# Row sums of three units on ScalarE, three exponential buffers, and normalising, products and shifts on GpSimd, in a two-layer attention and feed-forward kernel

## The reference, cut to what matters

```python
x = L0_attn_a_x                                   # (2, 1024, 512) float32, 2 batches
x = x + attn(layernorm(x), W_qkv_a, b_qkv_a, W_out_a, b_out_a)
x = x + ffn(layernorm(x), w_gate, w_up, w_down)
x = x + attn(layernorm(x), w_qkv_b, b_qkv_b, w_proj_b, b_proj_b)
x = x + ffn(layernorm(x), w_gate, w_up, w_down)   # the same weights again

def attn(x, ...):      # 16 heads of 32, causal
    q, k, v = split(x @ W_qkv + b_qkv)
    p = softmax(where(causal, q @ k.T * 32 ** -0.5, -inf))
    return (p @ v) @ W_out + b_out

def ffn(x, ...):       # hidden 2048
    return (silu(x @ w_gate) * (x @ w_up)) @ w_down

def layernorm(x):      # no scale, no shift, eps 1e-5
    return (x - mean(x)) / sqrt(var(x) + eps)
```

## Time and profile before

| | |
|---|---|
| median of 3 runs | 1995.39 us (1995.38 to 1996.1) |
| the profiled execution | 1995.06 us |
| its span, first to last instruction | 1993.3 us |
| mean granted TensorE clock | 0.999 |
| busy share TensorE, VectorE, GpSimd, ScalarE | 98%, 60%, 49%, 40% |
| attention part of iteration 0 | about 18 to 260 us |
| length of one iteration | 493 us |
| records of L1488 with values, with ones | 1536, 1024 |

### The profile page before, as it was taken

The page is one execution under the profiler, slowest core; times in us unless marked ns, Lnnn a source line. Parts: engine busy times, 40 slices in busy tenths (PEclk is TensorE's granted clock), DMA queues, the critical chain, the costliest instruction groups (busy, mean ns, idle before and its releaser), DMA issues.

```text
span 1993.3 us, 27851 instructions
## 1 busy us (share of the span) xinstructions
PE 1957.7 (98%) x10288; PEld 1438.2 (72%) x10288; DVE 1188.4 (60%) x2387; ACT 803.7 (40%) x1478; POOL 983.5 (49%) x767
## 2 busy tenths in 40 slices
PE   6999999999999999999999999999999999999999
PEld 5655588888765558888875656888887565688887
DVE  4777465445578845544567884545456777554544
ACT  2388532221248752222115874222211687332221
POOL 4025369763212537975421252897532225289740
PEclk9999999999999999999999999999999999999999
DMA  5334011121333301311252340111113234012111
GB/s 139 90 86 111 3 55 62 54 64 32 72 82 93 97 21 44 106 45 62 74 138 65 86 97 23 42 64 54 53 32 96 65 86 97 12 53 64 53 43 42
DMA packets 58821, 132.37 MB, mean 66 GB/s; under 512 B 10560, under 2 KB 11584, under 8 KB 58688
## 3 DMA queue, kind: packets, MB, share of 16 engines
q1 hardware_dynamic: 58688, 130.60, 24.3%
HBM read 75.51 MB, written 4.19 MB: 40 GB/s over the span
## 4 chain that ended last, share of the span: by engine, by line
PE 87%; DVE 6%; issue 4%; ACT 2%; POOL 1%; DMA 1%; SPq 0%; DVEq 0%; POOLq 0%; ACTq 0%
PE bank L1488 11%; PE bank L1354 10%; PE bank L1356 10%; PE bank L1355 10%; PE ring L1354 9%; PE ring L1356 9%; PE ring L1355 9%; PE bank L1461 8%; PE ring L1430 8%; PE ring L1345 1%; DVE xn L1051 1%; ACT kq_parts L844 1%; DVE stats L1014 0%; POOL area L657 0%; DVE xt_lo L1060 0%
## 5 line engine op out<-in xcount | busy, mean ns | idle before, releaser
L732 POOL TENSOR_SCALAR_AFFINE_SELECT prob<-prob 128x512 f32<-128x512 f32 x128 | 83.7, 654 | 509.5 <-ACT prob L861 379.2
L861 ACT ACTIVATE prob<-bank 128x512 f32<-128x512 f32 (+1 forms) x512 | 271.8, 572 | 135.0 <-PE bank L1461 125.2
L1168 DVE TENSOR_TENSOR x<-x,bank 128x512 f32<-128x512 f32 x256 | 170.5, 685 | 232.3 <-PE bank L1356 231.7
L657 POOL TENSOR_TENSOR area<-w_stage,area 128x1024 fp32r<-128x1024 f32 x126 | 302.1, 2398 | 10.5
L655 POOL TENSOR_SCALAR area<-w_stage 128x1024 fp32r<-128x1024 f32 x126 | 144.3, 1145 | 301.1 <-PE bank L1356 189.7
L1098 DVE CUSTOM_DVE_ANT_0 xn<-ring,mask_row 128x384 bf16<-128x384 f32 (+7 forms) x384 | 244.9, 661 | 70.1 <-PE ring L1430 65.7
L1354 PE MATMUL ring<-xt_hi,area 128*128 128x512 f32 x672 | 263.9, 393 | 1.3 <-DVE area L1201 1.3
L1356 PE MATMUL ring<-xt_hi,area 128*128 128x512 f32 x672 | 262.1, 390 | 0.0
L1355 PE MATMUL ring<-xt_lo,area 128*128 128x512 f32 x672 | 262.1, 390 | 0.0
L1461 PE MATMUL bank<-area 98*128 98x512 f32 (+3 forms) x768 | 233.2, 372 | 2.3 <-DMA area<-nm_lo 1.4
L1430 PE MATMUL ring<-area 96*128 96x512 f32 (+3 forms) x768 | 221.7, 360 | 2.9 <-DVE row_max L1098 2.1
(11 more groups left out here) (171 smaller groups left out, 3643.9 us busy)
## 6 DMA issues: line engine op xcount, KB each, us to landing
w_stage<-ffn_w SPq DMA_DIRECT2D x96, 512.0 KB, 3.5
area<-kq_parts SPq DMA_DIRECT2D x336, 128.0 KB, 2.4
w_stage<-attn_w SPq DMA_DIRECT2D x32, 512.0 KB, 4.8
area<-attn SPq DMA_DIRECT2D x48, 128.0 KB, 3.3
x<-x_in SPq DMA_DIRECT2D x16, 256.0 KB, 3.9
out<-x SPq DMA_DIRECT2D x16, 256.0 KB, 2.0
bias_rows<-row_bias SPq DMA_DIRECT2D x8, 256.0 KB, 4.2
masked<-x_in SPq DMA_DIRECT2D x6, 256.0 KB, 4.5
```

Of the source, the lines that this page charges most:

```text
L657: pool.tensor_tensor(lo, src, hi.bitcast(F32), ALU.subtract).then_inc(w_split, 1)
L861: act.activation(prob[:, step % PROB_BUFS, h, off:], scores_at(u, j, h), ACT.Exp, scale=SCALE).then_inc(prob_ready, 1)
L1168: dve.tensor_tensor(x[:, t, :], x[:, t, :], row_bank(s, n)[:, :], ALU.add).then_inc(rows_drained, 1)
```

## The change

- `SUMMED` gets unit 1: its row sums move from matmuls with ones to ScalarE, and `ORDER` has 62 instead of 68 letters v, `ACT_ORDER` 48 instead of 32 letters r, 16 of them for unit 1 in the first two strings.
- `PROB_BUFS` 2 to 3, `MASKED_BUFS` 3 to 2.
- The normalise steps of all but the first four tiles go to GpSimd, so do the shift (now four instructions) and the product with the reciprocals for all plain units but the last. In `POOL_ORDER` h is a shift, t a product; d now takes the next of deviations and normalise pairs.
- At the start each x tile has its own semaphore, variance and deviation come for two tiles at a time, the memset L767 stands behind them, and VectorE makes the low parts of the first two weight slots.
- `HEAD_OF_RING` begins with two value tiles instead of the first query and key projections. `EARLY` changes for units 1 and 5, and all strings are written anew.

```diff
-EARLY = {1: 2, 3: 12, 5: 9, 7: 12}
+EARLY = {1: 10, 3: 12, 5: 12, 7: 12}
...
-HEAD_OF_RING = (("q", 0), ("k", 0), ("v", 0), ("v", 1), ("ln1", 2), ("ln1", 3), ("q", 1), ("k", 1))
+HEAD_OF_RING = (("v", 0), ("v", 1), ("q", 0), ("k", 0), ("ln1", 2), ("ln1", 3), ("q", 1), ("k", 1))
...
-PROB_BUFS = 2
-SUMMED = (3, 5)
+PROB_BUFS = 3
+SUMMED = (1, 3, 5)
...
-    "pppppfffffffpfpppppfffffpppffpfpfpffpfpfpffpfpfpfpffpffpffpf",
...
+    "fffffpfppffpppppffffppfpfpffppfpffppfpfpffppfpfpffpfffffff",
...
-    "xxxxxxx",
-    "eexeeeeeeeeexe",
-    "eeeeoeeexeeeeeeeeereereererereereerreer",
...
+    "xxxxxxrrr",
+    "erererexrrexerreerrrrerreexeo",
+    "eeeexeeeeeeeeeereerreerreereereerreererxer",
...
-    "dbbwmmmbmmwmmbmmmmmwmmmbwmmmmmwbaaawammmambmmmbamammdmmwdw",
+    "bbddbdwwmbmbhmbmwbmmmtmmwmhmmbmmmmwtmmmhmaaamtmammmammmawtawdddmmmmdw",
...
-MASKED_BUFS = 3
+MASKED_BUFS = 2
...
-        x_loaded = [sem(f"x_loaded{c}") for c in range(CHUNKS)]
+        x_loaded = [sem(f"x_loaded{t}") for t in range(TT)]
...
+            def normalise_attn(it, u):
+                g, c = unit(u)
+                cols = slice(c * CHUNK, (c + 1) * CHUNK)
+                pool.wait_ge(recip_done, evacuations(it, u) * RECIPS)
+                pool.tensor_tensor(attn[:, g, cols], attn[:, g, cols], recip[:, :], ALU.mult).then_inc(attn_ready, 1)
+            def normalise_pair(it, ln, r):
+                if r >= 2:
+                    pool.wait_ge(ring_full, full(it, (f"ln{ln + 1}", r - 2)))
+                pool.wait_ge(rstd_ready, deviations(it, ln, 2 * r // CT))
+                for t in (2 * r, 2 * r + 1):
+                    src = x[:, t, :] if ln else source_tile(it, t)
+                    pool.tensor_scalar(xn_tile(t), src, mean_var[:, t, 0:1], rstd[:, t:t + 1], ALU.subtract, ALU.mult
+                                       ).then_inc(xn_ready, 1)
+            def shift(it, u):
+                least = row_max[:, u % 2, :]
+                pool.wait_ge(inverse_done, shifts(it, u))
+                pool.tensor_tensor(row_inv[:, :], row_inv[:, :], row_sum[:, :], ALU.mult)
+                pool.tensor_tensor(row_log[:, :], least, row_log[:, :], ALU.subtract).then_inc(shift_step, 1)
+                pool.wait_ge(shift_step, 2 * shifts(it, u) - 1)
+                pool.tensor_tensor(row_log[:, :], row_log[:, :], row_inv[:, :], ALU.subtract).then_inc(shift_step, 1)
+                pool.wait_ge(shift_step, 2 * shifts(it, u))
+                pool.tensor_scalar(least, row_log[:, :], 1.0, None, ALU.add).then_inc(shift_ready, 1)
...
+            for r in range(2):
+                pool.wait_ge(var_ready, r + 1)
+                t = slice(2 * r, 2 * r + 2)
+                pool.tensor_tensor(rstd[:, t], var_eps[:, t], minus_half[:, 0:2], ALU.pow).then_inc(rstd_ready, 1)
+            pool.wait_ge(rstd_ready, 2)
             pool.memset(k_stack[3 * HEAD:3 * HEAD + 2, 1:, :, :].bitcast(F32), 1.0).then_inc(ones_ready, 1)
             pool.wait_ge(ones_ready, 1)
-            inverse_deviation(0, 0, 0)
-            pool.wait_ge(xn_ready, CT)
-            for i in V_SLOTS:
-                hi, lo = w_part(i, slice(0, SLOT))
-                pool.wait_ge(w_hi_done, i + 1)
-                pool.tensor_tensor(lo, w_stage[:, i, :], hi.bitcast(F32), ALU.subtract).then_inc(w_split, 1)
+            pool.wait_ge(w_split, len(V_SLOTS))
...
-                deviations = iter(((0, 1), (1, 0), (1, 1)))
+                norms = iter((("deviation", 0, 1), ("pair", 0, 2), ("pair", 0, 3), ("deviation", 1, 0),
+                              ("pair", 1, 0), ("pair", 1, 1), ("deviation", 1, 1)))
+                shifted = iter(SUMMED)
+                divided = iter([u for u in PLAIN if ATTN_ON_POOL and u != UNITS - 1])
...
+                normalise_pair(it, 1, 2)
+                normalise_pair(it, 1, 3)
                 pool.wait_ge(xn_ready, it * 2 * TT + 2 * TT)
...
+            def first_normalise(r):
+                dve.wait_ge(rstd_ready, r + 1)
+                for t in (2 * r, 2 * r + 1):
+                    dve.tensor_scalar(xn_tile(t), x[:, t, :], mean_var[:, t, 0:1], rstd[:, t:t + 1],
+                                      ALU.subtract, ALU.mult).then_inc(xn_ready, 1)
+            def first_weights_lo(i):
+                hi, lo = w_part(i, slice(0, SLOT))
+                dve.wait_ge(w_hi_done, i + 1)
+                dve.tensor_tensor(lo, w_stage[:, i, :], hi.bitcast(F32), ALU.subtract).then_inc(w_split, 1)
...
-                        if n == RECIPS - 1:
+                        if n == RECIPS - 1 and (v_unit == UNITS - 1 or not ATTN_ON_POOL):
...
-            chunk_stats(0, 0)
-            normalise_pair(0, 0, 0)
-            normalise_pair(0, 0, 1)
+            for t in range(CT):
+                dve.wait_ge(x_loaded[t], 16)
+                tile_stats(t, x[:, t, :])
+                if t % 2:
+                    variances(t + 1, range(t - 1, t + 1))
+            first_normalise(0)
+            first_weights_lo(0)
+            first_normalise(1)
             xt_to_lo(0, 0, 0)
+            first_weights_lo(1)
             xt_to_lo(0, 0, 1)
```

112 lines of the change are left out of this document (50 added, 62 removed).

## The result

The changed kernel takes 2073.69 us (median of 4 runs, 2070.46 to 2075.42), the kernel before 1995.39 (1994.24 to 1996.1). The ratio is 1.0391, 95% interval 1.0374 to 1.0407: 78 us slower, where I had forecast 37 us faster with a range of 1930 to 1986.

What follows compares the result with a forecast made beforehand. TensorE, busy 98% of the span, was taken as the bound, so only removed TensorE work or stops could count. -25 - 4.5 - 6 - 5 + 4 = -36.5 us gave 1958.5 us, range 1930 to 1986.

Steps and rivals of the forecast that it cites:

- (c): Normalise steps moved from VectorE to GpSimd, at iteration heads and feed-forward entry: -6 us, ends -8.5 and +3.
- (a): Row sums of unit 1 leave TensorE, 256 of 1024 ones records: -25 us, ends -23 and -25.
- (e): Added work, mainly 64 row-sum tiles on ScalarE, hidden in the prologue and unit 0's stage: +4 us, ends 0 and +80.
- (b): The start: earlier statistics, deviations by two tiles, value tiles first in the ring: -4.5 us, ends -2 and -6.
- the first projection: Sign at the start: TensorE's first projection matmul near 13 us, where the kernel before has 17.98.
- (d): Three exponential buffers and a VectorE relieved of some 80 us, mostly in attention: -5 us, ends 0 and -40.
- slower: Rival, 9%: with two masked buffers VectorE's maxima wait for ScalarE's row sums; at 0.4 us a tile, about 2032 us.
- The rival on GpSimd's queue: Masks wait behind splits, products and shifts in GpSimd's in-order queue: 1975 to 1991 us, middle 1986; 15%.
- The fourth: Rival, 4%: ScalarE bounds unit 1's stage, TensorE only waits elsewhere; -25 becomes about -5 and nothing is measured.
- TensorE's busy time: Sign over the whole kernel: TensorE's busy time down by 25 to 30 us.
- the stops before the transposes: Sign at iteration heads: no stop of TensorE before transposes of over 0.3 us.
- TensorE's busy share falls while the span doesn't: Sign over the whole kernel by which the prediction would count itself wrong; no size given.

Runs made afterwards that it cites:

- the other kernel: The changed kernel with the normalise on VectorE, and the sums of unit 1 made a second time, unused, on TensorE: 2023.64 us against 2003.5 without them.
- the faster version: Changed kernel with normalise and products on VectorE, third unit's query pieces right behind mt0, one ScalarE exponential earlier: 1988.55 us, ratio 0.9967 to the kernel before.

## Why the prediction was wrong

**The step that failed is (c)**, "a tensor-scalar pass over 512 columns takes GpSimd 0.62 us". The row was of the right engine and size but of another form: its scalars are constants, those of the normalise differ by row. The pass takes 2.08 us. With it my own sum would have read 264.46 + 3.43 + 4.15 = 272.0 for the first pair against TensorE's 270.2, a stop, and a second pair 4.1 us behind it. -6 was +70, measured in both directions (70.2 and 69.3). Of the 70 us, 39 are in the longer waits for normalised rows (47.4 less the 4.7 and 3.8 of before). Some 24 us are TensorE's own instructions taking longer, at a lower mean clock (0.980 against 0.993). What masks that stand behind the passes in GpSimd's queue add, no run shows. The trace did not show the operation on GpSimd at all, so its price needed two ends, and I gave it one value.

**(a)** -25 was -20.1 on TensorE, and none of it was left as a gain. I had counted records by the distance to the next start of a group that stands alone; the runs' price per iteration is 5.0 us, where my ends were 5.7 and 6.3 and I took the upper one. This term was mis-sized by a little, but what was to cover its price was wrong altogether, the second step that failed: **(e)**, "room enough for 19.3", took ScalarE's idle time from 45 to 65 us for room. None of the 16 row sums could be done before mt0 (60.0 us), since of the scores that they read all but one tile stand behind it in the ring; the room was between mt0 and mt1, 19.9 us long with 6.9 us already used. The idle share of an engine is no room if what it shall do is not ready then. In the kernel before the sums came to +23; with the -20 measured in the other kernel that makes, as an estimate, 43 us for the row sums on ScalarE. In the changed kernel with the normalise undone, sums, order, buffers, products, shifts and start come to +8.4 together. Two small changes of the order around mt0 took 13 us off (2001.7 to 1988.6), so that a net gain of 0.3% is left of this change without its normalise and products on GpSimd.

**(b)** -4.5 was +2.3 for the new start with the old head of the ring. "The 5.21 us memset that ran before the deviation now runs behind it" stands in my text; I looked at what it delays on GpSimd and not at what it does to VectorE beside it. Without that, the new start in the kernel before is level with the old one (ratio 0.9994) and not 4.5 us better; the first projection comes at 16.8 there, at 16.5 in the changed kernel and at 14.5 in the faster version with the memset put back, not at 13.

**(d)** -5 for the buffers and the lighter VectorE: no run shows it apart. The product with the reciprocals and the shift on GpSimd are worth nothing that can be told. The 24.8 us that VectorE was to lose with the products rested on the mean of 1.24 us, of which 0.69 is VectorE's own price and the rest the wait beside GpSimd.

**Of the rivals**, slower had 9%, by the pair of masked buffers. VectorE waits for a masked tile 11.1 us in all in the changed kernel, far from the 0.19 us for each of 192 tiles from which it decides. The rival on GpSimd's queue named the right engine and the wrong work: masks, products and shifts, at 28 us, while the normalise passes were the load. The fourth, ScalarE bounding a stage so that the sums don't count, had 4% and was half right: on TensorE the sums did cost 20 us, but ScalarE's stage took them back. I had placed it at 105 to 125 us, and the stage was the one from 60 to 80 us.

**Of the signs**, the ones records (768), ScalarE's row sums (192) and VectorE's busy time (1104.6) came as forecast. TensorE's busy time, the first projection and the stops before the transposes did not, and "TensorE's busy share falls while the span doesn't" is what happened.

## What to carry to other kernels

Price a moved instruction by a row of the same engine and the same operand form, and where there is none, take the slowest form as the end of the range. Look at the single durations behind a mean before it is used as a price. Before idle time of an engine is called room, ask when the operands come and when the result is due: only the idle time between these two counts. An instruction whose result is needed only much later, such as this memset, belongs where the engine beside it has nothing to do.

## What the runs showed of the hardware

- **GpSimd's tensor-scalar pass over 128x512 float32**: 0.62 us with constants, 1.57 with one operand per row, 2.08 with two. VectorE's with two takes 0.54 (1.00 for two tiles) when GpSimd is still.
- **VectorE beside GpSimd**: the normalise of two tiles took 1.00 us alone, and 4.35, 4.7 and 5.97 us when begun beside a memset of 5.21 us, each ending some 0.7 us behind the memset. A pass over 128x2 took 2.91 us instead of 0.17 in the same way. It looks like waiting for the other, not like sharing. The Trainium skill (Trainium Architecture — The Big Picture, What this means for kernel authors) says that these two engines share a pair of ports with "an exclusive lock (not a bandwidth split)"; this trace agrees. But not every pair of instructions is held. A two-input pass of VectorE on 1,024 columns, begun at 9.24 beside the memset in the changed kernel, took 1.23 us, the same as at 15.84 without it (1.21), while the two-input product on 512 columns took up to 2.57 us instead of 0.69 beside GpSimd's weight split, which reads two inputs.
- **A stop can be dearer than its length**: behind the second of two stops (2.81 us) the eight transposes took 1.94 us instead of 1.06, the granted clock was 0.50 from 768 to 770 us and 1.00 from 775 on. Behind the first (2.32 us, 4.1 us earlier) they took 1.06.
